# A gated attention block on one core: the first attention and its feed-forward put into one block, with the last Wo chunks and two tiles' loads moved into the last batch, and the setup's pieces rearranged

## What is computed

```
x = x + tanh(g0) * A0(LN(x), ctx)     # 16 heads, 4 K/V heads of 96; keys are ctx (375 rows) and LN(x) itself
x = x + tanh(g1) * LN(x) @ W4.T       # W4 from 4-bit codes and scales, bf16
x = x + tanh(g2) * A1(LN(x), ctx)     # one head of 1024, values are ctx
x = x + tanh(g3) * (LN(x) @ W.T + b + low-rank part of a chosen rank)
A0: q = y Wq', k = [ctx, y] Wk', v = [ctx, y] Wv', softmax(q k / sqrt(96)) v, then Wo'
```

## Time and profile before

| | us |
|---|---|
| runs shown: median (lowest to highest of 3) | 2079.2 (2078.36 to 2084.17) |
| the profiled execution, its own time | 2077.89 |
| its span in the trace | 2076.1 |
| TensorE busy (matmuls) | 1978.1 (95%) |
| VectorE, ScalarE, GpSimd busy | 1036.8, 744.8, 735.1 |
| mean granted TensorE clock | 0.982 |

### The profile page before, as it was taken

One profiled execution on the slowest core, in us unless ns is written; L12 is line 12 of the kernel. 1 busy time (PEld: TensorE's weight loads), 2 busy tenths in 40 slices (PEclk: granted clock), 3 DMA queues, 4 the chain that ended last, 5 costly groups with the idle time before them and its releaser, 6 DMA issues. The chain is left out here.

```text
span 2076.1 us, 37357 instructions
## 1 busy us (share of the span) xinstructions
PE 1978.1 (95%) x13954; PEld 1302.7 (63%) x13968; DVE 1036.8 (50%) x1999; ACT 744.8 (36%) x1559; POOL 735.1 (35%) x722
## 2 busy tenths in 40 slices
PE   7989999998999999999999959999999968999998
PEld 3468888884666566666656525666666655666665
DVE  4555555533555555455555632433433446555564
ACT  3521111221555555555555640111111134444442
POOL 0000000110556666556666530110101146666662
PEclk9989999999999999999999989999999989999999
DMA  5533333333222222332222442323213356666562
GB/s 180 144 118 92 108 99 113 114 99 77 64 64 68 63 66 66 83 96 63 66 65 65 105 141 72 89 56 85 83 53 91 99 176 205 199 211 212 182 214 65
DMA packets 313217, 223.86 MB, mean 108 GB/s; under 512 B 247984, under 2 KB 284848, under 8 KB 308896
## 3 DMA queue, kind: packets, MB, share of 16 engines
q1 hardware_dynamic: 282560, 211.49, 35.2%
q10 hardware_dynamic: 30560, 11.02, 2.1%
HBM read 170.76 MB, written 51.65 MB: 107 GB/s over the span
## 5 line engine op out<-in xcount | busy, mean ns | idle before, releaser
L826 POOL TENSOR_TENSOR b_probT<-b_exp,b_probT 128x448 f16<-128x448 f32 (+2 forms) x256 | 266.6, 1044 | 297.3 <-ACT b_probT L889 297.2
L441 POOL TENSOR_TENSOR cT<-ctx_raw,cT 128x375 f16<-128x375 f32 x256 | 224.7, 898 | 132.4 <-ACT cT L436 132.4
L665 PE MATMUL a_pr<-a_yT,proj_q_p 128*128 128x256 f16 x2016 | 223.2, 273 | 0.0
L665 PEld LDWEIGHTS a_pr<-a_yT,proj_q_p 128*128 128x128 f16 x2016 | 197.2, 98 | 23.4
L1025 PE MATMUL b_kv_ps<-wkv_p,cT 128*128 128x384 f16 (+1 forms) x1152 | 210.8, 325 | 0.0
L1021 PE MATMUL b_kv_ps<-cT,wkv_p 128*128 128x375 f16 x1152 | 201.1, 326 | 3.7 <-PEq L458 3.7
L956 DVE TENSOR_REDUCE b_nmax<-b_mx_ps 112x2 f16<-112x974 f32 x128 | 149.6, 1169 | 106.7 <-PE b_mx_ps L1037 106.7
L1062 PE MATMUL b_s_ps<-b_qT,b_kT 96*128 96x448 f16 (+5 forms) x768 | 190.0, 355 | 2.2 <-DMA b_qT<-b_nrow 2.2
L1077 PE MATMUL b_o_ps<-b_probT,b_v 128*128 128x448 f16 (+5 forms) x768 | 187.2, 351 | 3.8 <-POOL b_probT L826 3.8
L887 ACT ACTIVATE b_exp<-b_s_ps 128x448 f32<-128x448 f32 (+2 forms) x256 | 137.8, 538 | 121.1 <-PE b_s_ps L1062 113.5
L1025 PEld LDWEIGHTS b_kv_ps<-wkv_p,cT 128*128 128x128 f16 (+1 forms) x1152 | 125.9, 109 | 71.1
(11 more groups left out here) (204 smaller groups left out, 2879.1 us busy)
## 6 DMA issues: line engine op xcount, KB each, us to landing
ctx_raw<-in_ctx_t SPq DMA_DIRECT2D x32, 1500.0 KB, 7.9
d_cn_raw<-in_ctx_nat SPq DMA_DIRECT2D x30, 512.0 KB
b_qT<-qk_scratch SPq DMA_DIRECT2D x32, 336.0 KB, 4.2
o_scratch<-b_o SPq DMA_DIRECT2D x128, 84.0 KB, 2.0
qk_scratch<-a_heads SPq DMA_DIRECT2D x70, 144.0 KB, 2.1
x_scratch<-c_x SPq DMA_DIRECT2D x14, 512.5 KB, 3.2
raw<-in_x SPq DMA_DIRECT2D x14, 512.0 KB, 3.7
c_x<-in_x SPq DMA_DIRECT2D x14, 512.0 KB, 3.3
```

Source lines behind the costliest of these rows:

```text
L441: pool.tensor_tensor(cT[:, p, 1, k, 0:S], ctx_raw[:, k, :], cT[:, p, 0, k, 0:S], ALU.subtract).then_inc(split_lo, 1)
L665: last = mm(pr[:, n % PR, 0:GT * P], w[:, b, k, at * P:(at + 1) * P], yT[:, g % 2, a, k, :], start=(x == 0 and k == 0), stop=(x == 2 and k ...
L826: pool.tensor_tensor(pT[0:m, c, 1, :], ex[0:m, i % 2, :], pT[0:m, c, 0, :], ALU.subtract).then_inc(p_lo, 1)
```

## The change

- Setup: 16 of the 48 projection pieces are split before the evictions start (ScalarE right behind the weights, VectorE behind its small work), four instead of six behind each later eviction. TensorE starts the high*high pass of the first chunk when the high halves are there (`w_hi`), and the other passes when the low ones are. The sum `c_col` is made after the normalisations.
- Projections: `tr` has a buffer for each tile of a group; `y_turned(t)` waits for `yT_low(t-2)`.
- First attention, first sequence: three blocks of K, then eight tops with nine matmuls behind each; VectorE takes V blocks after tops 2, 5 and 7.
- Wo: eight chunks in `wo_early`, four in `wo_late`, which now lies with `xin` in the space of the K and V projection weights (`wkv_p`, allocated at the outermost level). All twelve are split in the attention: chunks 0 to 7 at the odd steps of slot 14, 8 to 11 at steps 1, 4, 7, 10 of slot 15, loaded at steps 0, 1, 2, 4, ... 14 of slot 14 and 0, 2, 5 of slot 15, through two buffers.
- The blocks b and c are one: each engine runs its attention stream (now a function, `b_sync` and so on, bodies unchanged but for what the diff shows) and then its feed-forward stream. SyncE loads the rows and outputs of tiles 0 and 1 in slot 15, behind the last store of slot 14. W4 is loaded after the last store. Tile 13's load waits for all stores. Of tile 1's first half TensorE does eight chunks (24 matmuls) before it turns tile 0.
- `cn`, `wb_p` and W1 take other parts of the same space.

```diff
-KO_EARLY = 7
+KO_EARLY = 8
...
+        wkv_p = sb("wkv_p", [P, 2, KD, 2 * KW], F16)
...
-                        M_PIECES = 2 * KD
-                        PER_ROW = (len(pieces) - M_PIECES) // (2 * KD - BANKS)
+                    M_PIECES, EARLY_PIECES = 2 * KD, 16
+                    PER_ROW = (len(pieces) - M_PIECES - EARLY_PIECES) // (2 * KD - BANKS)
...
-                            for n in range(M_PIECES):
+                        for n in range(M_PIECES + EARLY_PIECES):
                             high(n)
...
+                        for n in range(M_PIECES, M_PIECES + EARLY_PIECES):
+                            low(n)
                         for i in range(2 * KD):
                             m, h = divmod(i, 2)
                             dve.wait_ge(m_hi, i + 1)
...
-                            for k in range(KD):
+                        pe.wait_ge(w_hi, 2)
+                        for i in range(BANKS):
+                            product(i, PASSES[0], 0, True, False)
+                        pe.wait_ge(w_lo, 2)
+                        for i in range(BANKS):
+                            for part in PASSES[1:]:
+                                product(i, part, 0, False, False)
+                        for k in range(1, KD):
                             pe.wait_ge(w_lo, 2 * (k + 1))
...
-                        tr = pb("a_tr", [P, 2, HALF], F32)
+                    tr = pb("a_tr", [P, GT, 2, HALF], F32)
...
-                                wait(pe, yT_lo, t)
+                            wait(pe, yT_lo, t - GT + 1)
...
+            wkv_flat = wkv_p.rearrange("p l k c -> p (l k c)")
+            WO_LATE = 2 * (KO - KO_EARLY) * D
+            wo_late = wkv_flat[:, 0:WO_LATE].rearrange("p (l k c) -> p l k c", l=2, k=KO - KO_EARLY)
+            xin = wkv_flat[:, WO_LATE:WO_LATE + 4 * D].bitcast(F32).rearrange("p (t c) -> p t c", t=2)
...
-                    wo_in = sb("b_wo_in", [P, D], F32)
+                wo_in = sb("b_wo_in", [P, 2, D], F32)
...
+                WO_SPLIT = [2 * n + 1 for n in range(KO_EARLY)] + [2 * KO_EARLY + 1 + 3 * n for n in range(KO - KO_EARLY)]
+                WO_LOAD = [0, 1] + [at + 1 for at in WO_SPLIT[:-2]]
...
+                FIRST_VALUES = (2, 5, 7)
...
+                        if isinstance(b, int) and b == B - 1:
+                            sp.wait_ge(kv_done, 6 * B)
+                            for t in range(2):
+                                load_x(sp, t, t)
+                            sp.wait_ge(split_hi, KD * B)
+                            sp.wait_ge(split_lo, KD * B)
+                            for i in range(2):
+                                sp.wait_ge(o_stored[i], 32 * (B - 1) * KV // 2)
+                            for t in range(2):
+                                load_tile(sp, t, t)
                         store(b, 0)
                         store(b, 1)
...
                     store(B - 1, 3)
-                        for i in range(2):
-                            sp.wait_ge(o_stored[i], 32 * B * KV // 2)
...
                     def wo_load(n):
-                            wait(act, wo_lo, n)
-                            act.dma_start(wo_in[:, :], wo[:, n, :]).then_inc(wo_loaded, 16)
+                        wait(act, wo_lo, n - 1)
+                        act.dma_start(wo_in[:, n % 2, :], wo[:, n, :]).then_inc(wo_loaded[n % 2], 16)
...
+                        if n >= KO_EARLY:
+                            act.wait_ge(kv_done, 6 * B)
...
-                        for k in range(4):
+                    for k in range(3):
                         block_low(0, 0, k)
-                        for t in range(4):
+                    for t in range(8):
                         top(0, t)
-                        block_low(0, 0, 4)
-                        for t in range(4, 8):
-                            top(0, t)
-                        block_low(0, 0, 5)
+                        if t in FIRST_VALUES:
+                            block_low(0, 0, 3 + FIRST_VALUES.index(t))
...
-                        for m in range(4 * BLOCK):
+                    for m in range(3 * BLOCK):
                         project(0, 0, m)
                     for t in range(8):
                         top_scores(0, 0, 0, t)
-                            for m in range(4 * BLOCK + 6 * t, 4 * BLOCK + 6 * t + 6):
+                        for m in range(3 * BLOCK + 9 * t, 3 * BLOCK + 9 * t + 9):
                             project(0, 0, m)
...
                 @block.sync
                 def _(sp):
+                    b_sync(sp)
+
+                    sp.wait_ge(wo_lo, KO)
+                    sp.wait_ge(scored, STEPS * B)
                     sp.dma_start(w4[:, :], w4_s[:, :]).then_inc(w4_loaded, 16)
...
-                    load(0, 0, 0)
-                    for k in range(KO - KO_EARLY):
-                        wait(sp, w_lo, k - len(stage) + 1)
-                        sp.dma_start(stage[k % 3][:, :], wo[:, KO_EARLY + k, :]).then_inc(w_loaded[k % 3], 16)
...
                 @block.tensor
                 def _(pe):
+                    b_tensor(pe)
+
+                    pe.wait_ge(kv_lo, kv_count(B - 1, 5))
+                    pe.wait_ge(wo_lo, KO)
...
                     def slot(j, p, s):
+                        ahead = KO_AHEAD if isinstance(s, int) and s == 1 else 0
+                        if ahead:
+                            out_proj(j, p, s, 0, 0, ahead)
+                            pe.wait_ge(o_read, KV * B)
...
                         if inside(s, TILES):
-                            out_proj(j, p, s, 0)
+                            out_proj(j, p, s, 0, ahead)
```

More of the change, by code:

```diff
@@ L753, in build, with row_pieces @@
+                    def row_pieces(i):
+                        first = M_PIECES + EARLY_PIECES + (i - BANKS) * PER_ROW
+                        return range(first, first + PER_ROW)
                     block = st.enter_context(nc.Block())
@@ L809, in _ @@
-                        run_slots(sp, slot, B)
-                        store(B - 1, 3)
-                        for i in range(2):
-                            sp.wait_ge(o_stored[i], 32 * B * KV // 2)
+                        for n, (src, _, _, runs, _) in enumerate(pieces):
+                            wait(sp, w_lo, n - RING + 1)
+                            if runs == 1 and len(src.shape) == 3:
+                                src = src.rearrange("p g d -> p (g d)")
+                            sp.dma_start(in_raw(n, runs), src).then_inc(loaded[n % RING], 16)
@@ new lines, in _ @@
+                        pe.wait_ge(m_lo, BANKS + 5)
+                        for n, (a, b) in enumerate(PASSES):
+                            for k in range(KD):
+                                last = mm(m_ps[:, 4, 0:1], bk_bc[:, a, k, :], bq_p[:, b, k:k + 1],
+                                          start=(n == 0 and k == 0), stop=(n == 2 and k == KD - 1))
+                        last.then_inc(b_done, 1)
+                retire_semaphores()
+                used += early
+                ctx_raw = whole.enter_context(nc.sbuf_tensor("ctx_raw", [P, KD, S], F32, side="right"))
```

1574 lines of the change are left out of this document (773 added, 801 removed).

## The result

| | before | after |
|---|---|---|
| runs: median (lowest to highest), us | 2079.11 (2078.36 to 2084.17, 4 runs) | 2042.35 (2041.09 to 2043.05, 4 runs) |
| ratio of the times, 95% interval | | 0.9817 (0.98 to 0.9834) |
| the profiled execution, us | 2077.89 | 2041.79 |
| its span, mean granted TensorE clock | 2076.1, 0.982 | 2040.0, 0.992 |

The kernel is 36.8 us faster, 36.1 by the two profiled executions; 2042.0 was forecast. The sum was right, but its term for the Wo chunks was 3 us too small, and surpluses of other stretches made up for it.

A forecast was written before the change was run, and what follows sets the result against it. TensorE, fully busy through the first attention's middle, was taken as the bound, with time to gain only at stage joins. Terms 1.7 - 4.9 - 4.2 - 1.8 + 2.4 - 29.4 = -36.2 from 2077.9 gave 2042 us; range 2036 to 2050.5.

The forecast's parts named there:

- Wo chunks: First attention's last two batches: five more chunks split there; plus 3.0 us in the last, minus 0.6 before; together plus 2.4.
- Setup, start and pieces: Setup: earlier first product minus 1.5 us, new wait at the ninth product 2.2, clock 1.0; together plus 1.7.
- The clock fear: Setup, behind the ninth product's wait: lost TensorE clock may cost 0 to 1.9 us, taken as 1.0.
- Setup, end, and first transposes: Setup's end: idle time before the transposes goes, minus 4.9 us; two transpose buffers and full clock, minus 4.2.
- First batch: First attention's start: nine matmuls behind each top cover waits for maxima; minus 1.8 us, between 0 and minus 2.8.
- The join: First attention's handover to the feed-forward: TensorE's waits for loads, chunks and norm go; minus 29.4 us, between minus 25 and minus 30.
- Rival 1: Last batch: five passes paid in full, 5.5 us instead of 2.4, exponentials 2 to 3 later; about 2048; chance 0.08.
- Rival 2: Join: outputs still come late, the 12.45 us load wait and slow matmuls (1.7) stay; 2056 us; chance 0.06.
- rival 4: Last batch: moved loads choke SyncE's queue and stores wait; kernel slower than before, ending 6 us later; chance 0.02.

The follow-up runs named there:

- the mended order: The changed kernel with chunks 9 and 10 of Wo split one step earlier, same work in all; last batch 27.20 us, 2045.55 us in all.
- the late loads: The changed kernel with the first two tiles' outputs and rows loaded behind the attention's last store, not in the last batch; 2059.21 us.

## Why the prediction was right, and where it was wrong

- **Setup, start and pieces.** +1.7 was forecast, +1.5 came, and the closeness is luck. The forecast was -1.5 for the start, +2.2 for the wait, +1.0 for the clock behind it. Measured were -1.2, +1.14 and nothing; the +1.5 are seven more slow matmuls at the very start than the first profile of the kernel before had, and against its second the line is +0.1. The pace of the pieces was reckoned well: the ninth product was forecast at 56.9 us, and with sixteen early pieces it began between 57.0 and 57.6 in eight profiles of nine. Its wait was 1.1 to 2.2 us, by when the eighth had ended. The clock fear came true once: behind the 2.21 us of the run with the old first batch it was 0.81 and 0.77 in the next 8 us, and the second 192 products took 43.26 us instead of 41.61. Behind 2.12 and 2.14 us (the mended order, the late loads) it stayed at 1.00, so of three such waits one brought it. Without early pieces the bias products start 2.7 us sooner, which is the price of the term.
- **Setup, end, and first transposes.** -4.9 and -4.2 were forecast, -5.0 and -4.4 came, for the reasons given: idle 5.51 to 0.52 us, clock 0.50 to 1.00, transposes of both tiles in 1.94 us. Without early pieces 7.3 of these 9.4 us came back (35.1 us from the first bias product to the second group of projections, 27.86 after); the second `tr` buffer was not tested by itself. The -5.0 depends on the execution, too: in four of the eleven variants these bias products ran at a clock of 1.00 and the stretch took 14.9 us, not 16.6.
- **First batch.** -1.8 was forecast, -2.2 came, -2.0 by the experiment. A further -1.65 behind it was not forecast and isn't the change's.
- **Wo chunks: the step that failed.** The last batch grew by 6.0 us where the term had 3.0 (the last but one gave 0.9 for 0.6). "Five passes could add 5 x 1.21 = 6.1 less the 2.0 us that GpSimd idles" took GpSimd as the bound and ScalarE's passes at nothing, since ScalarE was busy only 17.11 of 23.9 us. The runs say otherwise: VectorE's passes are worth 3.5 us (near the 3.0), ScalarE's 1.2 once VectorE's are gone, and 1.3 remain with both cut, in which are the loads' issues and the five short passes, up to 2.13 us long. Moving 3.7 us of work from GpSimd to VectorE gives nothing clear of scatter; mending the order of VectorE's queue gives 1.0. By the forecast's own marks the batch took 30.15 us where about 27 stood, and "a last batch over 30 us" was one of its signs of being wrong. The rows read as a ring of exponential, low part, scores and output over four engines with two buffers, in which idle time of an engine is not room; no run changed the number of buffers, so this reading fits all the runs but is not shown. Rival 1 (5.5 and a further 2 to 3 us of late exponentials) had a chance of 0.08. Its late exponentials are to be seen; its size, some 8 us with what the last but one gives back, lies as far above the measured 5.1 as the forecast's 2.4 lies below. The total shows nothing of the error, because the clock (-1.65) and small surpluses of the other stretches gave 3 us that no term had.
- **The join.** -29.4 was forecast, -29.5 came, or -28.2 against the second profile of the kernel before, which is inside the forecast's -25 to -30; agreement to 0.1 us is partly luck. The late loads bring back 15.0 us of it, the missing early matmuls 5.9; the weights' load was issued at 1213.70, 7 us before the forecast's 1221, and nobody waited for it. Rival 2 is out (no wait), and of rival 4 only the form was seen: 5.51 us of issue that stores stood behind, with no wait put down to them.
- **The total.** 2042.0 forecast, 2042.35 measured. The closeness is luck in part: an error of +3 us on the last batch met errors of -3.3 us on other lines. Two slips in the working moved nothing: a product takes 84.46 / 16 = 5.3 us, not 5.2, and the slow matmuls behind the join's wait cost 6.41 - 4.70 = 1.7 us, not 1.9.

## What to carry to other kernels

Bound a stage's added work by the chain of its engines, not by the busiest one: list for each added instruction what stands behind it in its queue and who waits for that, and treat idle time between dependent steps as already spent. At joins the reckoning by what the tensor engine must still do came within 1.2 us of either profile of the kernel before; loads belong where the queue reaches them a landing time ahead, with other matmuls over the norm. And check each term against its own stretch: a total that comes out right can hide terms that don't, a mark that one profile gives can move by 1.5 us in the next, and a gain of 2 us may not be seen in a total behind a stretch with a falling clock.

## What the runs showed of the hardware that was not expected

- A VectorE pass of 8 columns took 0.17 us and 2.13 us, though both came 0.1 us before a GpSimd pass ended and had a further one ready behind it; one of 1024 columns took 1.21 us undisturbed and up to 3.18. Cutting ScalarE's work made the batch 2.1 us *longer*; the rows show VectorE's passes moved into GpSimd's.
- The first matmuls of the program start 0.43 us apart and then 0.21, and how many are 0.43 us apart differs between executions of one kernel: 7 and 14, worth 1.5 us, under a granted clock that reads 1.00 in both.
- The granted clock of the same stretch differs between executions: 0.63 and 1.00 between 508 and 512 us in two profiles of the kernel before; 0.90 and 1.00 in the bias products, worth 1.7 us; 0.70 to 0.80 at the second handover. Together they make single profiles scatter by 2 us and more, which is as much as most terms of this study.
